# Evicting x_in of a Mamba block once, in 128 rows, and building both channel groups by four SyncE DMAs

## The reference

```
xz = x @ Wi.T + bi                      # 256 -> 1024: x_in (512 channels) and z (512)
u  = silu(causal_conv4(x_in) + conv_b)  # per channel, over tokens t-3 .. t
dt = softplus(x_in[..., :32] @ Wdt.T + bdt)
h[t] = h[t-1] * exp(dt * A) + dt * Bm * u   # 16 states per channel
y  = sum over the states of h * Cm
out = (y * silu(z)) @ Wo.T + bo + x * mean(Dv)
```

## The kernel before

| copies of block | after | before |
|---|---|---|
| 0 | x(3) | repd(0), second half |
| 1 | repw(0), second half | x(2), then the loads wa(20) to wa(27) |
| 2 | wa(27) | repd(1, q=0..3), then repw(1, q=0..3) |
| 3 | repw(2, q=1) | repw(2, q=2) |
| 4 | x(5), behind repw(3, q=1) | repw(3, q=2) |
| k = 5, 6, 7, 10, 11, 13, 14, 15 | repw(k-1, q=1), or a store behind it | repw(k-1, q=2) |
| 8 | repw(7, q=3) | wa(52) |
| 9 | repw(8, q=0) | repd(8, q=0..3) |
| 12 | repw(11, q=3) | a store |

## Time and profile before

### The profile page before, as it was taken

One profiled execution on the slowest core, in us unless ns is written; L12 is line 12 of the kernel. 1 busy time (PEld: TensorE's weight loads), 2 busy tenths in 40 slices (PEclk: granted clock), 3 DMA queues, 4 the chain that ended last, 5 costly groups with the idle time before them and its releaser, 6 DMA issues. The chain is left out here.

```text
span 760.1 us, 8303 instructions
## 1 busy us (share of the span) xinstructions
PE 644.2 (85%) x2928; PEld 333.1 (44%) x2928; DVE 666.6 (88%) x450; ACT 607.4 (80%) x1074; POOL 293.8 (39%) x184
## 2 busy tenths in 40 slices
PE   7867786799896999979798999994977997798857
PEld 5632333364342466445144575531231553265435
DVE  2437947879999999999999999999999999999971
ACT  2488896879889989998788989898888787866663
POOL 0107020134344588479912565046970060600010
PEclk9997998989997899999899999997997999899879
DMA  8431465341838070431658070614234331605001
GB/s 294 148 138 43 164 225 164 133 172 32 320 104 315 7 245 5 160 117 49 227 150 301 34 236 0 231 47 166 84 146 132 139 111 71 206 28 221 1 1 55
DMA packets 40026, 103.08 MB, mean 136 GB/s; under 512 B 4080, under 2 KB 13040, under 8 KB 39984
## 3 DMA queue, kind: packets, MB, share of 16 engines
q1 hardware_dynamic: 37424, 94.40, 34.2%
q10 hardware_dynamic: 2560, 8.14, 4.6%
HBM read 23.08 MB, written 4.19 MB: 36 GB/s over the span
## 5 line engine op out<-in xcount | busy, mean ns | idle before, releaser
L1124 ACT ACTIVATE G<-RD,COL 128x1024 f32<-128x1024 f32 (+1 forms) x288 | 280.0, 1042 | 56.2 <-PE Y L1424 50.8
L1246 DVE TENSOR_TENSOR_SCAN G<-G,STT,RV 128x1024 f32<-128x1024 f32 (+1 forms) x160 | 312.5, 2016 | 1.5 <-ACT G L1124 1.5
L1246 DVE TENSOR_TENSOR_SCAN G<-G,RV 128x1024 f32<-128x1024 f32 (+1 forms) x128 | 268.7, 2155 | 13.9 <-ACT G L1124 13.8
L1424 PE MATMUL Y<-G,RW 128*32 128x512 f32 x1024 | 144.6, 682 | 49.4 <-DVE G L1246 46.1
L849 POOL TENSOR_SCALAR LV<-LV 128x4 f32<-128x4 f32 x18 | 17.3, 962 | 226.4 <-ACT XN L944 226.1
L858 POOL TENSOR_TENSOR LV<-LV,HALF 128x4 f32<-128x4 f32 (+1 forms) x25 | 47.8, 1913 | 135.8 <-DVE LV L1201 134.3
L1424 PEld LDWEIGHTS Y<-G,RW 128*32 128x32 f32 x1024 | 28.0, 117 | 127.6 <-DVE G L1246 64.6
L875 POOL TENSOR_SCALAR XN<-X,LV 128x256 f32<-128x256 f32 x36 | 75.9, 2113 | 1.9
L1391 PE MATMUL MB<-XI,DIAG 128*64 128x512 f32 x248 | 64.3, 656 | 12.7 <-DMA XI<-XI 10.8
L1350 PE MATMUL MB<-MT,XF 128*128 128x256 f32 x240 | 59.6, 393 | 9.9 <-ACT MT L986 7.6
L1369 PE MATMUL MB<-XT,WI 128*128 128x512 f32 x128 | 63.4, 624 | 3.7 <-ACT XT L970 3.7
(11 more groups left out here) (96 smaller groups left out, 779.7 us busy)
## 6 DMA issues: line engine op xcount, KB each, us to landing
RD<-DW SPq DMA_DIRECT2D x60, 512.0 KB, 3.7
RV<-DW SPq DMA_DIRECT2D x60, 512.0 KB, 4.9
W<-in_w SPq DMA_DIRECT2D x48, 256.5 KB, 3.6
XI<-XI ACTq DMA_DIRECT2D x30, 256.5 KB, 5.6
X<-in_x SPq DMA_DIRECT2D x8, 512.0 KB, 6.3
out<-X SPq DMA_DIRECT2D x7, 512.0 KB, 3.3
G<-in_w SPq DMA_DIRECT2D x4, 513.0 KB, 8.4
RV<-in_w SPq DMA_DIRECT2D x4, 513.0 KB, 12.3
```

The source lines that it names most:

```text
L1124: eng.activation(G[:, i % NG, t0:t1], RD[:, q, t0:t1], ACT.Exp, scale=NAC[:, states(i):states(i) + 1]).then_inc(sems["exp"])
L1246: eng.tensor_tensor_scan(g, g, RV[:, (4 * k + q) % NR, t0:t1], STT[:, idx:idx + 1] if goes_on else 0.0, ALU.mult, ALU.add).then_inc(sems[" ...
L1424: ins = eng.matmul(Y[32 * q:32 * q + 32, 512 * h:512 * h + 512], RW[:, states(i + o), :], G[:, (i + o) % NG, 512 * h:512 * h + 512], start ...
```

## The change

For all blocks but 6, 10 and 14 (`direct`), "halo" and "xi" no longer write to `XI`. They write x_in of all 128 channels into one buffer of `ZS` (`inner`), which has three more columns for it: that of block k - 1, or for the first block of an iteration its own (`lent`). The gates of that block go there only later, once the convolution has been done. Each "xi" is one ScalarE instruction of 128 partitions. "sh" moves from ScalarE to SyncE, at the same place in the order, and for these blocks it has four DMAs: for each group of 64 channels one straight and one shifted copy from `ZS` to `XI`. Blocks 6, 10 and 14 keep their evictions and their two DMAs, which SyncE now issues too. Where the buffer of `ZS` has been used before, halo waits for the last output projection that reads it. The first convolution of block 0 reads `ZS` with full matmuls of 128 rows. The planner's ScalarE cost of "xi" goes from 52 to 31.

```diff
--- before.py
+++ after.py
@@ -30,7 +30,7 @@
     "sh": lambda k: "sh",
     "col": lambda: "col", "mask": lambda: "mask", "wi": lambda: "wi", "wdt": lambda: "wdt", "bo": lambda: "bo", "wo": lambda: "wo",
 }
-STEP = {"sh": 32}
+STEP = {"sh": lambda k: 32 if direct(k) else 64}
 
 
 EMPTIES = {"xt": "xtc", "fm": "ffn", "fi": "ffn", "xim": "xi", "xdm": "xd", "um": "u", "zm": "z", "dm": "dt", "opa": "op", "dvm": "dvs", "mt": "mtc"}
@@ -40,7 +40,7 @@
 
 LOAD = {"xt": (19, 0), "mm": (38, 0), "mt": (19, 0), "fm": (95, 0), "xim": (76, 0), "xdm": (25, 0), "um": (76, 0), "zm": (76, 0),
         "dm": (38, 0), "opa": (96, 0), "opm": (96, 0), "red": (76, 0), "exp": (0, 48), "sum": (0, 60), "sq": (0, 60),
-        "xtc": (0, 25), "ms": (0, 35), "mtc": (0, 25), "ffn": (0, 30), "op": (0, 30), "xi": (0, 52), "xd": (0, 17), "u": (0, 30),
+        "xtc": (0, 25), "ms": (0, 35), "mtc": (0, 25), "ffn": (0, 30), "op": (0, 30), "xi": (0, 31), "xd": (0, 17), "u": (0, 30),
         "z": (0, 30), "dtr": (0, 25), "dte": (0, 48), "dtl": (0, 48), "silu": (0, 57), "expset": (0, 57),
         "save": (0, 10)}
 RATE, STORE = 240, 100
@@ -103,6 +103,16 @@
     return c < 4 or c >= 22
 
 
+def direct(k):
+
+    return k % 4 == 2 and k > NZ
+
+
+def lent(k):
+
+    return k - 1 if k % 4 else k
+
+
 def made(stage, c):
 
     return ("v" if early(c) else "") + stage
@@ -154,7 +164,7 @@
 
     def __call__(self, stage, *item):
         sem = DMA[stage](*item) if stage in DMA else stage
-        self.total[sem] = self.total.get(sem, 0) + (STEP.get(stage, 16) if stage in DMA else 1)
+        self.total[sem] = self.total.get(sem, 0) + (STEP.get(stage, lambda *a: 16)(*item) if stage in DMA else 1)
         self.value[stage, item] = self.total[sem]
         self.now += 1
         self.sem[stage, item] = sem
@@ -356,6 +366,8 @@
         it = k // 4
         zs = gates(k)
         yield from after(("xtc", 6 * it + 2, 1), ("xtc", 6 * it + 3, 1), ("um", k - 1, 1))
+        if lent(k) >= NZ and not direct(k):
+            yield from after(("opm", (lent(k) - NZ) // 4, 1, 3))
         yield 1
         do("halo", k)
         do("xim", k, 0)
@@ -686,7 +698,7 @@
         STT = sb("STT", [P, 64])
         LV = sb("LV", [P, 6, 7, 4])
         DW = sb("DW", [P, 2, TOK])
-        ZS = sb("ZS", [P, NZ, TOK])
+        ZS = sb("ZS", [P, NZ, TOK + 3])
         RD = sb("RD", [P, 4, TOK])
         RV = sb("RV", [P, NR, TOK])
         G = sb("G", [P, NG, TOK])
@@ -729,6 +741,10 @@
         def tokens(c):
             it, ph, hf = c // 6, c % 6 // 2, c % 2
             return it, ph, hf, X[:, (2 * it + hf) % NX, :, :], LV[:, c % 6, :, :], XN[:, place[c] % 2, :, :]
+
+        def inner(k):
+
+            return ZS[:, lent(k) % NZ, :]
 
         def fourfold(v):
 
@@ -803,6 +819,22 @@
                     tiles = slice(2 * pairs[0], 2 * pairs[-1] + 2)
                     ov = out[512 * g:512 * g + 512, :].rearrange("(i p) d -> p i d", p=P)[:, tiles, :]
                     eng.dma_start(ov, X[:, g % NX, tiles, :]).then_inc(sems[DMA["store"](g)], 16)
+                elif stage == "sh":
+                    k, = a
+                    e.wait_ge("halo", k)
+                    e.wait_ge("xi", k, 1)
+                    if direct(k):
+                        for g in range(2):
+                            eng.dma_start(XI[64 - 64 * g:128 - 64 * g, g, 0:TOK + 2],
+                                          XI[64 * g:64 * g + 64, g, 1:TOK + 3]).then_inc(sems["sh"], 16)
+                        return
+                    if k:
+                        e.wait_ge("um", k - 1, 1)
+                    c0 = 512 if k in HALVED else 0
+                    for g in range(2):
+                        same, other = slice(64 * g, 64 * g + 64), slice(64 - 64 * g, 128 - 64 * g)
+                        eng.dma_start(XI[same, g, c0:TOK + 3], inner(k)[same, c0:TOK + 3]).then_inc(sems["sh"], 16)
+                        eng.dma_start(XI[other, g, c0:TOK + 2], inner(k)[same, c0 + 1:TOK + 3]).then_inc(sems["sh"], 16)
                 elif stage == "repd":
                     k, q, p = a
                     t0, t1 = span(k, p)
@@ -1030,28 +1062,29 @@
                         for hf in range(2):
                             e.wait_ge("um", k - 1, hf)
                     e.wait_ge("half")
+                    if lent(k) >= NZ and not direct(k):
+                        e.wait_ge("opm", (lent(k) - NZ) // 4, 1, 3)
                     src = HAL[:, k % 4, :] if k // 4 % 2 else ZERO[:, :]
-                    eng.activation(XI[:, :, 0:3], src.unsqueeze(1).broadcast_to([P, 2, 3]), ACT.Copy
-                                   ).then_inc(sems["halo"])
+                    if direct(k):
+                        eng.activation(XI[:, :, 0:3], src.unsqueeze(1).broadcast_to([P, 2, 3]), ACT.Copy
+                                       ).then_inc(sems["halo"])
+                        return
+                    eng.activation(inner(k)[:, 0:3], src, ACT.Copy).then_inc(sems["halo"])
                 elif stage == "xi":
                     k, hf = a
                     e.wait_ge("xim", k, hf)
                     if hf and k // 4 % 2 == 0:
                         eng.activation(HAL[:, k % 4, :], bank("xim", k, hf)[:, 509:512], ACT.Identity,
                                        bias=COL[:, BI + k % 4:BI + k % 4 + 1])
-                    for g in range(2):
-                        ps = slice(64 * g, 64 * g + 64)
-                        ins = eng.activation(XI[ps, g, 3 + 512 * hf:515 + 512 * hf], bank("xim", k, hf)[ps, :],
-                                             ACT.Identity, bias=COL[ps, BI + k % 4:BI + k % 4 + 1])
-                    ins.then_inc(sems["xi"])
-                elif stage == "sh":
-                    k, = a
-                    e.wait_ge("halo", k)
-                    e.wait_ge("xi", k, 1)
-                    c0 = 512 if k in HALVED else 0
-                    for g in range(2):
-                        eng.dma_start(XI[64 - 64 * g:128 - 64 * g, g, c0:TOK + 2],
-                                      XI[64 * g:64 * g + 64, g, c0 + 1:TOK + 3]).then_inc(sems["sh"], 16)
+                    if direct(k):
+                        for g in range(2):
+                            ps = slice(64 * g, 64 * g + 64)
+                            ins = eng.activation(XI[ps, g, 3 + 512 * hf:515 + 512 * hf], bank("xim", k, hf)[ps, :],
+                                                 ACT.Identity, bias=COL[ps, BI + k % 4:BI + k % 4 + 1])
+                        ins.then_inc(sems["xi"])
+                        return
+                    eng.activation(inner(k)[:, 3 + 512 * hf:515 + 512 * hf], bank("xim", k, hf), ACT.Identity,
+                                   bias=COL[:, BI + k % 4:BI + k % 4 + 1]).then_inc(sems["xi"])
                 elif stage == "xd":
                     it, hf = a
                     ps = slice(32 * hf, 32 * hf + 32)
@@ -1378,10 +1411,8 @@
                         e.wait_ge("diag0")
                         e.wait_ge("halo", 0)
                         for t in range(4):
-                            for g in range(2):
-                                ps = slice(64 * g, 64 * g + 64)
-                                ins = eng.matmul(bank("um", 0, 0)[ps, :], DIAG0[ps, t, ps], XI[ps, g, t:t + 512],
-                                                 start=(t == 0), stop=(t == 3))
+                            ins = eng.matmul(bank("um", 0, 0), DIAG0[:, t, :], inner(0)[:, t:t + 512],
+                                             start=(t == 0), stop=(t == 3))
                         ins.then_inc(sems["um"])
                         return
                     e.wait_ge("diag")
```

## The result

The changed kernel takes 785.0 us (median of 4 runs, 783.01 to 786.57) against 761.2 for the kernel before on the same chip (758.97 to 765.12). The ratio is 1.031, 95% interval 1.026 to 1.036: 3.1% slower, 23.8 us. The forecast was 763.3 with a range up to 775, so the time lies outside it. The profiled execution has a span of 783.4 us.

The account below looks back on a forecast made before the run. It took VectorE's scans as the bound from 207 to 702 us and ScalarE's chain before 167 us. Terms +0.5, +4.2, +0.5 and -2.2 gave +3.0 us: 763.3 us, range 757 to 775.

Parts of the forecast that it names:

- step 5: Block 9: copies ahead of block 8's dt replications make ScalarE later, between 0 and 1.5 us, taken as +0.5.
- step 3: Block 2: copies hold block 1's replications; its first scan starts at 126.6, +8.2 us, shrinking to +0.5 at 166.56.
- step 4: Block 4: copies hold the last two w replications of block 3, delaying its third scan by 4.2 us.
- step 6: Relief: two later VectorE waits follow ScalarE stretches with some 2.5 us less work: -2.2 us, bounds 0 and -4.
- Evictions: 13 of 16 blocks evict each half once; 26 ScalarE instructions of 0.68 us go, 17.7 us.
- The copies' issue: SyncE issues the copies at ScalarE's 0.56 us each: 2.2 us for four, other end 3.7.
- Step 1: Second half of block 0: ScalarE gets ahead of the second dt by 0.7 to 1.8 us, taken as 1.0.
- Step 2: Block 1: copies hold the load of x group 2; ScalarE's chain and VectorE's 10.19 us wait grow by 3.1 us.
- Slow landings: Rival: behind 1 MB of copies a replication lands in 9.2 us, not 4.9: +15.2 us, 775.5; chance 0.17.
- Holds cost nothing: Rival: replications and loads are not held behind the copies, so only relief remains: 754.2 us; chance 0.12.
- Planner: Rival: the lower planned eviction cost may move steps and copies in the order: 757 to 769 us; chance 0.10.
- Not what it says: Rival: 128-row evictions cost 1.36 us, so ScalarE saves only its issues: 764.5 us; listed as no effect, 0.03.

Follow-up runs that it names:

- e7: The changed kernel with only block 9's copies later in SyncE's order, behind block 8's dt replications and one of w: 777.1 us, ratio 1.020.
- e8: The changed kernel without the last four loads of FFN weights, everything else of SyncE's order kept: 778.8 us, ratio 1.024.
- e2: The kernel before with its two shift copies of each block issued by SyncE, evictions and bytes as before: 779.2 us, ratio 1.025.
- e3: The changed kernel with the copies of blocks 1, 2, 4 and 9 later in SyncE's order, all else kept: 761.0 us, ratio 1.002.
- e10: The kernel before with its two copies per block issued by SyncE, those of blocks 1, 2, 4 and 9 later in the order: 756.2 us, ratio 0.992.
- e9: The changed kernel with the planner's cost of an eviction put back from 31 to 52: 784.4 us, ratio 1.029.
- e12: The changed kernel with only block 2's copies later in SyncE's order: 788.1 us, ratio 1.034.
- e1: The changed kernel with its copies (four or two a block) issued by ScalarE again, at the same place in the order: 788.0 us, ratio 1.034.

## Why the prediction was wrong, point by point

**The mechanism was right at the four places, its sizes were not, and at block 9 it stopped a step short.** The forecast named the four places, and only those show new waits for DMA: the 22.7 us for `RV` are 13.35 at block 1, 7.59 at block 3, and 1.13 and 0.58 at block 8. Blocks 7, 11 and 15 have none, as put. What was wrong is what each costs. The span grew by 23.3 us where the sum has 3.0. Of the 20.3 that are missing, 8.6 are step 5's, 6.3 step 3's and 3.7 step 4's; the other 1.7 lie in step 6 and behind 488 us.

**Evictions**: right. 52 instructions of 676 ns became 26 of 675 ns, 17.6 us of ScalarE against 17.7 forecast. Rows cost no time here.

**The copies' issue**: the term "2.2 us for four" failed. Four took 3.2 us (0.50, 0.60, 0.65, 1.34 and the gaps), near the other bound of 3.7. And the issues right behind them were slower too, which had no term: the four replications of `dt` took 5.23 us instead of the 3.39 of the earlier trace rows.

**Step 1**: right. The second `dt` of block 0 came 1.1 us earlier, apart from a start-up difference of 1.2 us.

**Step 2**: forecast +3.1, measured +7.1. x was issued at 93.86 (forecast 93.3) but landed 5.9 us later, not 3.6: ScalarE resumed at 99.83 instead of 97. In these 5.9 us the DMA engines moved 1.48 MB at 250 GB/s, namely the rest of the copies, x, and the first weight loads issued behind it; in the 3.6 us before it was 1.04 MB at 286 GB/s. The Trainium skill (DMA: Bandwidth & Descriptors, Anatomy of one DMA) gives, for a DMA that GpSimd issues, the variable part as bytes over 436e9. By it the 0.44 MB more are 1.0 us, an estimate, which is less than half of the 2.3 measured: both measured rates are well under that figure. The other 1.2 us is the sentence that "their products end before the later ScalarE chain asks for them". They didn't: the FFN product waited until 100.55 and took 3.56 us at a granted clock of 0.55, and the reduction behind it in TensorE's order released the exponentials at 105.17, 1.43 us after ScalarE had come to them. With the 2.00 us that the products took before, the reduction would have ended near 103.6, an estimate, and ScalarE was ready at 103.74; so it was the clock, for which the forecast had no term, that made this sentence false.

**Step 3**: forecast 126.6, measured 134.11. Of the 7.5 us too little, 3.9 came in with ScalarE's lateness from step 2, 1.1 from the copies' issue, 1.9 from the replications' issue and 0.6 from the landing (5.5). The waits of 3.46 and 5.51 us swallowed 8.9 of it, and then there was none left; that "each us more at the first scan is paid in full" was nearly right, 7.5 us more at 134 being 6.3 more at 173. The forecast sat at the edge of the slack, where each small term that was taken low came out whole.

**Step 4**: forecast +4.2, measured 7.6. The copies and the landing took 3.3 + 5.5 = 8.8 us instead of 7.1, and ScalarE's last eviction began 1.9 us ahead of the due scan (217.01 against 218.88) instead of 3.7. What made it later against the scans I did not trace.

**Step 5**: forecast +0.5, measured about 9 by the table and 8 by e7. This is the largest miss, and this step failed in its reasoning too. It followed the `dt` replications to their exponentials and stopped. Behind them in the queue stood the four FFN weight loads, which went out at 426.25 instead of 409.78, and on TensorE their products stand ahead of a reduction that the next exponentials need: without these loads 7.3 of the 9 us are gone (e8). Steps 2 and 5 share this fault: a transfer was called harmless because its own reader has time, though the reader's engine, in order, has not.

**Step 6**: forecast -2.2. Of its two waits the first fell from 1.49 to 0.39 us and the second, 0.67 us, is gone: 1.8. A new wait of 0.90 us for ScalarE at 582.50 takes half of that back.

**The rivals.** *Slow landings* came nearest with 775.5, but not by its mechanism: landings were 5.5 to 5.9 us, not 9.2, and blocks 7, 11 and 15 were untouched. *Holds cost nothing* is refuted by e2, and with it, for queues that wait, the rule of the Trainium skill (Trainium Kernel Development and Optimization, Key Constraints) that issuing from several engines "only saves the sequencer's issue time": moving two issues a block from one queue to another cost 18.9 us. Once the holds are gone, the time was 761.0 (e3), not 754.2; e10, with one pair of copies, is at 756.2, so the second pair has a price that this rival left out. *Planner* is out by e9. *Not what it says* is out by the 675 ns.

**The chances.** 0.74 on within 1% took the slack as safe. Every bound that the text kept on a cost (issue 0.9, landing above 4.9, step 5 at 1.5) lay on the late side, and those of steps 2 and 3 feed the same chain, so they add up rather than average out. The range should have been the chain at its upper bounds, not the forecast plus one of them. Even that would not have held step 5, whose bound of 1.5 us stood against 9.

## What to carry to other kernels

Before a DMA that waits for a late event is moved to an in-order queue, list what stands behind it there, and for each of these what stands behind its reader on the reader's engine: that second step held most of block 9's part (5.4 us by e8's ratio, 7.3 by its profile) and 1.2 us of block 1's. If the move is worth having, move the place in the order with it (here four places, 24 us). A delay that is to be swallowed by later waits needs them to belong to another chain; where the same late event feeds both, the waits stay and nothing is swallowed (e12). And compare an experiment with the kernel that it was made from: lateness against the kernel before hides what the change also gives.

## What the hardware showed that I had not expected

- The issue time of a DMA grew with what was still in flight: 0.5, 0.6, 0.65 and 1.3 us for four of 256 KB on an empty queue, then 1.3 us each for the 512 KB ones behind, which had taken 0.85 each before. Four copies of half that size in block 0 took 0.51, 0.60, 0.60 and 0.61. Right behind eight replications the first copy took 1.16 (e12). On ScalarE's queue, with SyncE's transfers in flight, four took 7.7 us (e1).
- A 512 KB load behind 1 MB of on-chip copies landed in 5.9 us. Before it had taken 3.6, behind four replications of 256 KB each.
- A matmul that has waited long for a load is slow as well: the granted clock was 0.59 over the wait from 92.00 to 100.50 and 0.55 over the products behind it, 3.56 us for what takes 2.00 at 1.00.
